# A four-layer graph network on one core: one-hots compared from PSUM, attention's products and sums partly in PSUM, and the last layer in one stage

## The reference

```python
deg = jnp.maximum(segment_sum(ones, dst), 1.0);  norm = deg ** -0.5
x = x + attention(h, edge_attr, ...)       # layer 0
x = x + segment_sum(h[src], dst)           # layer 1
x = x + relation_conv(h, src, dst, rel)    # layer 2, two passes
x = x + channels(h, norm, src, dst, ...)   # layer 3

# layer 0, aggregation: 4 heads of 64 columns, a weight per edge and head
msg = out_j * alpha[:, :, None];  out = segment_sum(msg, i).mean(1) + bias
# layer 2, each pass
hw = einsum('nd,rdh->nrh', h, W); agg = segment_sum(hw[src, rel], dst) / deg; h = relu(agg)
# layer 3
low  = relu(lin_self(feat))      + mean_agg(relu(lin_neigh(feat)) * norm)
high = relu(lin_self_high(feat)) - mean_agg(relu(lin_neigh_high(feat)) * norm)
identity = relu(lin_id(feat))
att = softmax(sigmoid([low@a_l, high@a_h, identity@a_m]) @ W_att.T / 3)
rst = 3 * (att0 * low + att1 * high + att2 * identity)
```

## Time and profile before

| | us |
|---|---|
| median of 3 runs (lowest, highest) | 14033.08 (14031.82, 14033.41) |
| the profiled execution, its own time | 14016.92 |
| its span, first to last instruction | 14015.4 |
| GpSimd busy | 8457.6 (60% of the span) |
| VectorE busy | 7365.5 (53%) |
| TensorE busy | 7345.0 (52%) |
| ScalarE busy | 3395.4 (24%) |

### The profile page before, as it was taken

One profiled execution on the slowest core, in us unless ns is written; L12 is line 12 of the kernel. 1 busy time (PEld: TensorE's weight loads), 2 busy tenths in 40 slices (PEclk: granted clock), 3 DMA queues, 4 the chain that ended last, 5 costly groups with the idle time before them and its releaser, 6 DMA issues. The chain is left out here.

```text
span 14015.4 us, 154885 instructions
## 1 busy us (share of the span) xinstructions
PE 7345.0 (52%) x27414; PEld 5002.7 (36%) x27414; DVE 7365.5 (53%) x15655; ACT 3395.4 (24%) x7069; POOL 8457.6 (60%) x8196
## 2 busy tenths in 40 slices
PE   4577767776777772035551297333333533333387
PEld 4344444444444441025551033333333333333233
DVE  6688888888888884647772002222223222222301
ACT  0244444444444442036661001000000100000100
POOL 1366666666666662877777501777776477777300
PEclk9888888888888886556665698555555655555588
DMA  1344444444444448036661285111111311111065
GB/s 23 91 140 143 141 142 144 139 145 140 143 140 142 140 142 65 10 105 181 182 182 53 85 294 190 25 26 25 26 25 24 128 26 26 26 26 26 11 243 212
DMA packets 1037353, 1462.78 MB, mean 104 GB/s; under 512 B 518414, under 2 KB 733934, under 8 KB 1011937
## 3 DMA queue, kind: packets, MB, share of 16 engines
q1 hardware_dynamic: 651986, 1075.95, 24.6%
q0 software_dynamic: 284800, 382.51, 10.2%
q10 hardware_dynamic: 100368, 2.41, 0.8%
HBM read 946.06 MB, written 512.36 MB: 104 GB/s over the span
## 5 line engine op out<-in xcount | busy, mean ns | idle before, releaser
L1522 POOL DMA_INDIRECT l2s_got<-rel_d,l2s_idx x3232 | 3252.5, 1006 | 1899.4 <-POOLq L1519 1006.0
L1548 PE MATMUL l2s_ps<-l2s_got,l2s_oh 128*128 128x65 f32 (+1 forms) x6464 | 1473.2, 421 | 2797.5 <-PEq L1546 2790.4
L873 PE MATMUL edge_z<-edge_w,edge_feats 128*128 128x512 f32 x3232 | 2092.0, 735 | 877.7 <-PEq L870 877.7
L1548 PEld LDWEIGHTS l2s_ps<-l2s_got,l2s_oh 128*128 128x128 f32 x6464 | 1409.0, 330 | 2863.0 <-issue 2863.0
L793 POOL DMA_INDIRECT rows_d<-edge_rows,edge_place x1624 | 1657.3, 1021 | 1100.1 <-POOLq L791 661.4
L1223 DVE TENSOR_TENSOR net_acc<-net_acc,l2s_ps 128x65 f32 (+1 forms) x3232 | 720.4, 223 | 2735.8 <-DVEq L1570 1877.4
L1241 POOL DMA_INDIRECT count_d<-all_list_val,all_list_idx x1568 | 1821.0, 1161 | 503.4 <-issue 464.2
L785 POOL DMA_INDIRECT edge_gath<-h_d,edge_idx x1624 | 1652.9, 1018 | 495.0 <-issue 494.7
L1354 PE MATMUL at_ps<-at_msg,at_oh 128*128 128x128 f32 x3520 | 746.3, 399 | 879.8 <-PEq L1350 863.3
L876 PE MATMUL edge_z<-edge_products,edge_oh_dstT 128*128 x3232 | 1155.5, 445 | 0.0
L876 PEld LDWEIGHTS edge_z<-edge_products,edge_oh_dstT 128*128 128x128 f32 x3232 | 737.4, 228 | 1010.2 <-issue 1010.2
(11 more groups left out here) (364 smaller groups left out, 10171.3 us busy)
## 6 DMA issues: line engine op xcount, KB each, us to landing
at_rows<-rows_d SPq DMA_DIRECT2D x444, 528.0 KB
count_d<-edge_zero SPq DMA_DIRECT2D x202, 994.0 KB
l1s_cnt<-count_d SPq DMA_DIRECT2D x49, 1600.0 KB, 6.3
l3s_cnt<-count_d SPq DMA_DIRECT2D x49, 1600.0 KB, 6.3
rel_d<-l2t_out SPq DMA_DIRECT2D x100, 768.0 KB, 3.3
l1s_cnt<-count_d SPq DMA_DIRECT2D x49, 1536.0 KB, 6.0
l3s_cnt<-count_d SPq DMA_DIRECT2D x49, 1536.0 KB, 6.0
edge_drow<-loc_d SPq DMA_DIRECT2D x203, 256.0 KB
```

The source lines that it names most:

```text
L873: pe.matmul(z[p % 2][:, t, :], feats[q][:, j * P:(j + 1) * P], w[:, :], start=True, stop=False, skip_group_check=True)
L1522: pool.indirect_dma_start(out=got[r][:, j, 0:cols], out_offset=None, in_=table, in_offset=bass.IndirectOffsetOnAxis(ap=idx[i][:, k:k + 1], ...
L1548: ins = pe.matmul(ps[q][:, j, 0:wide], oh[q][:, j, :], got[r][:, j, 0:wide], start=True, stop=True)
```

## The change

**Attention.** VectorE makes the one-hots in one operation of 1024 columns, by comparing an iota that it copied into PSUM with `loc`; ScalarE keeps only its list copies. The weights are copied into PSUM (`wts_ps`, 32 columns), the products are made in two operations of 1024 columns, one into SBUF (`wtd`) and one into PSUM (`wtd_ps`), and `msg` is the sum of the two. `prepare` is split: `weigh` (up to the products) stands ahead of the additions, `messages` between the first and the second addition. **Relation layer:** the one-hots read the iota from PSUM. **Last layer:** the three blocks are one. TensorE makes the linear maps of block b+2 while it accumulates source block b in the first half of the targets; the mix of a half runs as soon as that half's sums are there. The lists of counts are freed after layer 1, and the normalised features of the last layer stay until its end.

```diff
@@ attention_sum
-        wtd = [t.sb(f"wtd{q}", [P, G, OUTJ]) for q in TWO]
+        wtd = t.sb("wtd", [P, G, 2 * D])
+        wtd_ps = t.ps("wtd_ps", [P, G, 2 * D])
+        wts_ps = t.ps("wts_ps", [P, GS, SPAN, HEADS])
+        iota = t.ps("iota", [P, P])
...
-                    for n in range(G):
-                        ins = s.activation(far[q][:, n, :], net.iota[:, :], ACT.Square, bias=loc[q][:, n:n + 1])
-                    ins.then_inc(squared, 1)
-                    s.wait_ge(squared, 1).then_inc(squared, -1)
-                    s.activation(oh[q][:, :, :], far[q][:, :, :], ACT.Relu, bias=1.0, scale=-1.0).then_inc(onehot, 1)
...
                         pe.wait_ge(messaged, 1).then_inc(messaged, -1)
-                        pe.wait_ge(onehot, 1).then_inc(onehot, -1)
...
+                    v.tensor_copy(wts_ps[:, :, :, :], wts[r][:, :, :, :]).then_inc(kept, 1)
+                    v.wait_ge(placed, 1).then_inc(placed, -1)
+                    v.tensor_tensor(oh[q][:, :, :], iota[:, None, :].to_broadcast([P, G, P]),
+                                    loc[q][:, :].unsqueeze(2).to_broadcast([P, G, P]), ALU.is_equal)
+                    v.wait_ge(kept, 1).then_inc(kept, -1)
+                    for half, out in ((0, wtd), (1, wtd_ps)):
                         ins = v.tensor_tensor(
...
-                        prepare(w0 + GS, 1 - q, (r + 1) % 4)
+                        weigh(w0 + GS, 1 - q, (r + 1) % 4)
                         v.wait_ge(blk_listed, 1).then_inc(blk_listed, -1)
+                        blocks = item_values(nc, v, blk[q], NBU * P)
+                        v.sem_inc(blk_free, 1)
                         v.wait_ge(summed, 1).then_inc(summed, -1)
-                        add_items(net, v, acc, blk[q], added, lambda j: ps[q][:, j, :], 2 * D)
-                        v.sem_inc(ps_free, 1)
-                        v.sem_inc(blk_free, 1)
+                        with Scratch(nc, v):
+                            here = acc[:, bass.ds(blocks[0], 2 * D)]
+                            v.tensor_tensor(here, here, ps[q][:, 0, :], ALU.add).then_inc(added, 1)
+                        messages(1 - q)
+                        v.wait_ge(added, 1).then_inc(added, -1)
+                        with Scratch(nc, v):
+                            here = acc[:, bass.ds(blocks[1], 2 * D)]
+                            v.tensor_tensor(here, here, ps[q][:, 1, :], ALU.add).then_inc(ps_free, 1)
@@ gather_sum
-                    v.tensor_tensor(oh[q][:, :, :], net.iota[:, None, :].to_broadcast([P, G, P]),
+                    v.tensor_tensor(oh[q][:, :, :], iota[:, None, :].to_broadcast([P, G, P]),
@@ channel_layer (new, in place of channel_tables, dense_sum and channel_mix)
+                for b0, b1 in halves:
+                    blocks = used(b1) - b0
+                    cols = blocks * P
+                    for b in range(NBU):
+                        pe.wait_ge(loaded[n % RING], 16).then_inc(loaded[n % RING], -16)
+                        for c in range(0, cols, 512):
+                            if c == 3 * 512 and b0 == 0 and b + 2 < NB:
+                                turn_row(b + 2)
+                            ins = pe.matmul(ps[:, c:min(c + 512, cols)], table[:, b, :],
+                                            cnt[n % RING][:, c:min(c + 512, cols)], start=b == 0, stop=b == NBU - 1)
...
+                        if b0 == 0 and b + 2 < NB:
+                            products(b + 2)
...
+                tables()
+                v.wait_ge(mix_loaded, 64)
+                for b0, b1 in halves:
+                    sums(b0, b1)
+                    mix(b0, b1)
```

More of the change, by code:

```diff
@@ L1379, in _ @@
                 done = net.v_done.of(v)
+                v.tensor_copy(iota[:, :], net.iota[:, :])
                 done(v.memset(acc[:, :], 0.0))
-                prepare(0, 0, 0)
+                weigh(0, 0, 0)
+                messages(0)
                 with Loop(nc, v, GROUPS) as it:
@@ L1578, in _ @@
                         v.memset(got[r][:, :, cols:wide], 1.0)
+                done(v.tensor_copy(iota[:, :], net.iota[:, :]))
                 done(v.memset(acc[:, :], 0.0))
@@ L1805, in _, with turn_row @@
-                pe.wait_ge(weights_loaded, 160)
-                turn(0)
-                with Loop(nc, pe, NB // 2):
-                    for q in TWO:
-                        pe.wait_ge(copied, 1).then_inc(copied, -1)
-                        turn(1 - q)
-                        pe.wait_ge(scaled, 1).then_inc(scaled, -1)
-                        pe.matmul(ps[q][:, :], ht[q][:, :], ws[:, :], start=True, stop=True).then_inc(done, 1)
+                def turn_row(b):
+                    if b:
+                        pe.wait_ge(scaled, 1).then_inc(scaled, -1)
+                    pe.transpose(row, norm.blocks[:, b, :], net.ident[:, :]).then_inc(row_turned, 1)
@@ new lines, in _ @@
+            @block.scalar
+            def _(s):
+                for b in range(NB):
+                    s.wait_ge(done, 1).then_inc(done, -1)
+                    s.activation(own[:, b, :], product[:, 0:3 * D], ACT.Relu).then_inc(kept, 1)
+                for _ in halves:
+                    s.wait_ge(logits, 1).then_inc(logits, -1)
+                    s.activation(lg[:, :, :], lg[:, :, :], ACT.Sigmoid).then_inc(squashed, 1)
+                    s.wait_ge(shifted, 1).then_inc(shifted, -1)
+                    s.activation(at[:, :, :], at[:, :, :], ACT.Exp).then_inc(raised, 1)
@@ L1836, in _ @@
                         v.wait_ge(kept, 1).then_inc(kept, -1)
[L1837 to L1838 removed]
+                        v.tensor_scalar(table[:, b, :], product[:, 3 * D:5 * D], 0.0, net.isqrt[:, b:b + 1], ALU.max,
                                         ALU.mult).then_inc(scaled, 1)
[L1841 to L1848 removed]
@@ new lines, in sums @@
+                def sums(b0, b1):
+                    blocks = used(b1) - b0
+                    cols = blocks * P
+                    v.wait_ge(summed, 1).then_inc(summed, -1)
+                    v.tensor_copy(turn[:, 0:cols], ps[:, 0:cols]).then_inc(moved, 1)
+                    for k0 in range(0, blocks, some):
+                        k1 = min(k0 + some, blocks)
+                        v.wait_ge(turned, 1).then_inc(turned, -1)
+                        got = tp[:, 0:(k1 - k0) * wide].rearrange("p (k w) -> p k w", w=wide)
+                        own_done(v.tensor_copy(target[:, b0 + k0:b0 + k1, 0:wide], got))
+                        v.sem_inc(taken, 1)
```

257 lines of the change are left out of this document (131 added, 126 removed).

## The result

| | before | after |
|---|---|---|
| median (lowest, highest) of 4 runs, us | 14032.45 (13999.49, 14033.41) | 13457.42 (13448.18, 13463.62) |
| ratio, 95% interval | | 0.9595 (0.9579, 0.9612) |
| profiled execution, span | 14016.92, 14015.4 | 13463.62, 13462.0 |

A forecast was written before the change was run, and what follows sets the result against it. Bounds were taken per stage: GpSimd's lists in attention, long gathers in the relation layer, three successive blocks in the last. Gains 110 + 174 + 200 = 484 us off 14016.9 give 13533, plus 16 a median of 13549; 8-in-10 range 13465 to 13690.

The forecast's parts named there:

- Here the new order costs: Attention, TensorE: the new order makes a loop through two engines; pitch 5.89 us, end 7420, block 110 us earlier.
- The loop through TensorE: Attention: message 1.23, TensorE's start 0.49, 16 records 3.75, to the addition 0.30, to the next message 0.22: 5.99 us.
- rival B: Attention: TensorE's loop is as long as a gap of 1.02 us makes it; -6 there, 13665 us in all; 12%.
- My sum of 5.49: Attention, VectorE: its operations and semaphore wait per group add up to 5.49 us, 5.6 with the loop's branch.
- Relation layer: One-hot's iota in PSUM: gathers no longer lengthened by VectorE's second SBUF operand; 174 us over both passes, bounds 0 and 180.
- Last layer: One stage in place of three blocks: end at 13815 against 14015.4, 200 us gained, between 145 and 220.
- 0.83 us per moved transpose and product: Last layer, first half: time each of the 48 moved transposes and products adds on TensorE; 40 us, bounds 24 and 95.
- The cover: Last layer: three accumulating matmuls' 2.6 us hide the chain's first piece; failing that, about 1 us per block, 48 in all.
- Rival C: Last layer: the mixed stream loses TensorE's clock or its cover; 13854 us in all; 4%.
- Rival D: Attention: PSUM operands run at half rate, a pitch of 9.9 us; slower, 14429 us in all; 3%.
- attention's 173: Attention, GpSimd: 30 lists at 41.55 us end at about 7358, 173 us earlier, the most the block can give.
- the forecast's own range: Total for the forecast as worked out (73%): 13465 to 13640 us, from attention's 173 and last layer's 220 to 60 and 145.

## Why the prediction was wrong in size and right in kind

**Attention, the step that failed.** "Here the new order costs" gave a pitch of 5.89 us and an end at 7420, 110 us earlier. The loop through TensorE exists and its form was right, but the times in it and the share of groups that it rules were not. Measured are 5.63 us and 7363:
- From the message's end to TensorE 0.30 us and not 0.49: the wait for the one-hots is gone from TensorE's path (the run with one more wait: 0.45). The loop was 1.22 + 0.30 + 3.75 + 0.30 + 0.24 = 5.81 instead of 5.99. The 0.30 that I had chosen between 0.15 and 1.02 was measured as such, and with it rival B fell.
- VectorE's own loop is 5.37 us (`loc` to `loc`, 6503.75 to 6509.12 in the timeline) and not 5.6. My sum of 5.49 was 0.12 too long: large operations follow each other every 1.13 to 1.14 us (6509.43, 6510.57, 6511.70), not every 1.16. The 0.11 for the branch don't show.
- TensorE set the pitch in 60% of the groups (the view of waits has 130 of some 217 first additions), where I had taken 74% from the granted clock. The granted clock is 0.60 now, below the 0.63 of before, so it isn't that. A burst may take 5.37 - 1.22 - 0.30 - 0.30 - 0.24 = 3.31 us before VectorE has to wait, and the bursts lie between 2.5 and 3.76 us: 121 of the 220 take 3.6 or more, 77 less than 3.31. I had split them into all at 1.2 GHz, by the granted clock, and all far shorter; here none is as short as the shortest of before, 2.02 us, and yet 77 are short enough.

0.60 x 5.81 + 0.40 x 5.37 = 5.63 is the measured pitch; of its 220 single values 116 lie at 5.8 and 87 at 5.4. The difference of 0.26 over 220 groups is 57 us, and the end is 7363. That is also where GpSimd is ready (7361): the block gave 170.5 of the 173 that were possible. "Here the new order costs" also had the wrong sign: the order with the message between the additions gains 172 us over the order with the message first (the run above).

**Relation layer.** 178.7 us against 174. That the second SBUF operand is the cause is shown by the run that puts it back (164 of 177 us on the same stretch) and by the absence of an effect of the order. The Trainium skill, page "SBUF — State Buffer", section "Who interferes with whom", has it that an instruction with two SBUF inputs contends with a GpSimd instruction that reads SBUF, and one with a single SBUF input does not. By that rule, the traces agree here: the longest gather is 2003 ns with two and 992 with one. Its inference that a tensor_tensor leaves descriptor generation alone is against these runs: such operations lengthened indirect transfers from 0.95 to up to 2.0 us.

**Last layer.** 211.3 us against 200. The two blocks ahead took 6.9 us (8.3 forecast, from a window of 208 us that the earlier trace rows does not show; by the earlier trace rows the table pass took 215.1), the first half 296.4 (305), moving out 18.2 and 16.7 (18.2 and 16.5), the second half 255.6 (254.7), the mix 39.0 (39.4), the store 5.5 (7). The term that was off is the 0.83 us per moved transpose and product: measured it is (296.4 - 265.1) / 48 = 0.65. The clock stayed at 0.99, and the records there are 0.27 us for a transpose and 0.44 for each of two products, 1.15 in all, which overlap with their neighbours. The cover held: TensorE was busy 296.80 of 297 us. Rival C fell.

**PSUM operands.** Rival D fell: the one-hot takes 1.23 us, the products 1.21 and 1.22 with the output in SBUF and in PSUM, the message 1.22.

**Profiled execution and median.** I added 16 us, as before; the changed kernel's profiled execution was its slowest of four, 6 us above the median. That is 22 of the 92 us between forecast and result; attention is 60, the last layer 11, the relation layer 5, less the 7 of the later start and between the stages. All terms of the sum erred to the same side, and the range had too little room at its lower end, where it held attention's 173 and the last layer's 220 but not the 22. The upper end of the forecast's own range is a slip: with 60 and 145 it comes to 14033 - 379 = 13654, not 13640; nothing hangs on it.

## What to carry to other kernels

Where GpSimd issues indirect transfers all the time, look for VectorE operations with two SBUF operands beside them, and put one operand in PSUM. For VectorE that is free here (a message of 1024 columns takes 1.22 us with one operand in PSUM and 1.23 with none), and the two stages that it relieves gave 349 of the 560 us. What it is worth is read from the transfers' lengths beside those operations, not from their columns. When a new order adds a wait, write down every gap of the old order too (an operation behind its own input, two additions in a row): in the old order they can lie under another wait, and in the new one they may be what the order covers. And at a point where two engines are even, a pitch wrong by under 5% makes a term of 170 into one of 110, so work out the length of a loop from its own path, wait by wait.

## What the runs showed of the hardware

What a VectorE operation with two SBUF operands costs GpSimd's indirect transfers is not a constant, and not proportional to its columns (the operations have 1024 columns where nothing else is said):

| case | us of GpSimd per group |
|---|---|
| relation layer, one one-hot, two kernels | 0.41 and 0.44 |
| relation layer, a second one behind it | 0.12 more |
| attention, the message alone | 0.54 |
| attention, two products alone | 0.65 |
| attention, one-hot, two products and message | 1.87 |
| attention before, four products of 512 columns and a message: (1427.7 - 1254.7) / 221 | 0.78 |

The traces show on what it depends: on where in VectorE's operation a transfer starts. A transfer that starts while the operation runs is longer by what is left of the operation, less 0.12 us; one that is already under way when the operation starts is not longer. In the earlier trace rows the one-hot runs from 9502.86 to 9504.09. The gather at 9503.32 has 0.77 us of it left, 0.95 + 0.77 - 0.12 = 1.60, and 1.60 is its length. The gather ahead of it, in the same timeline, had begun before the one-hot and ends after its start:

```profile
9502.06 0.95 POOL L1522 DMA_INDIRECT l2s_got<-rel_d,l2s_idx  x1 [0.30 <-issue]
```

In attention with all operands in SBUF, the one-hot of 6500.47 ends at 6501.70, and the transfer at 6501.19 comes to 0.97 + 0.51 - 0.12 = 1.36 (1.34 in the trace); the one at 6502.84, 0.10 behind the start of a product, to 0.97 + 1.12 - 0.12 = 1.97, as in the trace. With an operation counted as running from 0.05 us behind its start, this gives all transfers' lengths within 0.06 us but for 2 of 3224 in the relation layer before, 1 of 3225 with the iota put back, 2 of 3226 with two one-hots, none of 646 with all of attention's operands in SBUF, none of 866 with the message alone and 1 of 849 with the products alone. Attention before, with its four short products in a row, is less regular: 118 of 901 are off. Where one operand lies in PSUM there is nothing of it: 992 ns at the longest in the relation layer, 998 in attention. GpSimd's list copies are held too: the copy into `counts_list_val` takes 1.20 us in the mean with all of attention's operands in SBUF, 0.21 in the changed kernel.

So the price is a matter of phase. A second one-hot directly behind the first costs little because the transfer that the first one held runs on into the second, and the next starts when little of the second is left. The four operations of attention's group follow each other so closely that 643 of the 646 transfers beside them are held. Which part of a transfer is held, the read of its indices or another, was not tested.

What stays at a fixed size is small: a satisfied wait on TensorE costs 0.15 us, and an operation of VectorE that waits for the one directly ahead of it starts 0.24 to 0.30 us late.
